# Experts run in two parts, the first on twelve quads' tokens from the end of the attention on

## The reference, cut to what matters

```python
x = x + xattn(layernorm(x), ctx)              # (64, 128, 128), 16 heads of 8
y = layernorm(x)                              # 8192 tokens
scores = softmax(y @ gate_w.T)                # 8 experts
sel = top_k(scores + expert_bias, 2)
for each chosen (token, expert e):
    r = y[token] * scores[token, e]
    out[token] += (silu(r @ w1[e]) * (r @ w3[e])) @ w2[e]     # 128 -> 352 -> 128
x = x + out
```

## Time and profile before

| | us |
|---|---|
| median of 3 runs | 871.06 |
| the profiled execution | 866.23 |
| its span | 864.2 |
| TensorE busy | 720.2 |
| GpSimd busy | 437.7 |
| VectorE busy | 494.9 |
| ScalarE busy | 419.3 |

### The profile page before, as it was taken

How to read it: one execution, slowest core, us unless ns; L and a number is a source line. 1 busy time by engine, 2 the same in 40 slices (tenths; PEclk the granted TensorE clock), 3 DMA queues, 4 the chain that set the end, 5 groups by cost and what they waited for, 6 DMA issues and landing times.

```text
span 864.2 us, 24903 instructions
## 1 busy us (share of the span) xinstructions
PE 720.2 (83%) x7007; PEld 577.8 (67%) x7008; DVE 494.9 (57%) x1404; ACT 419.3 (49%) x935; POOL 437.7 (51%) x779
## 2 busy tenths in 40 slices
PE   1689999999999999999963359999999999999800
PEld 1356677666777776676642158989999899898800
DVE  2446667675777776777743425555555555554536
ACT  1246677676677776776551024444444444443300
POOL 6311127665667675665566724555555545445510
PEclk9969999998999999999995769999999999999965
DMA  2445455565666656655300112212121222212179
GB/s 57 142 118 144 130 143 157 136 178 164 162 174 162 169 135 159 164 153 157 75 27 32 59 34 58 59 55 58 58 61 52 59 57 55 61 52 58 38 268 315
DMA packets 99774, 94.84 MB, mean 110 GB/s; under 512 B 15015, under 2 KB 89385, under 8 KB 99632
## 3 DMA queue, kind: packets, MB, share of 16 engines
q1 hardware_dynamic: 82832, 72.81, 31.5%
q0 software_dynamic: 8416, 16.86, 5.7%
q10 hardware_dynamic: 8448, 4.20, 1.6%
HBM read 55.00 MB, written 39.26 MB: 109 GB/s over the span
## 4 chain that ended last, share of the span: by engine, by line
PE 59%; DMA 12%; issue 9%; SPq 6%; DVE 6%; POOL 5%; ACT 2%; DVEq 0%; POOLq 0%; ACTq 0%
PE m_b L1190 7%; PE score_b L999 7%; PE u_b L1039 6%; PE score_b L957 4%; PE turned_b L1021 4%; PE score_b L198 3%; POOL expert_rows L440 3%; DMA head_rows<-qk 2%; SPq L236 2%; DVE nm L530 2%; PE m_a L1180 2%; PE turned_b L200 2%; PE turned_b L199 2%; PE score_b L200 2%; PE turned_b L198 2%
## 5 line engine op out<-in xcount | busy, mean ns | idle before, releaser
L471 POOL DMA_INDIRECT expert_results<-v,where x135 | 132.9, 984 | 156.8 <-DMA expert_results<-v,where 133.7
L530 DVE TENSOR_REDUCE nm<-score_b 128x8 f32<-128x960 f32 x128 | 148.2, 1158 | 96.4 <-PE score_b L999 92.8
L440 POOL DMA_INDIRECT expert_rows<-rows,places x128 | 128.9, 1007 | 71.0 <-POOL rows L434 49.7
L842 ACT ACTIVATE pT<-turned_b 120x1024 f32<-120x1024 f32 x128 | 130.9, 1023 | 61.2 <-PE turned_b L1021 46.4
L921 ACT ACTIVATE v<-score_b 128x352 f32<-128x352 f32 x135 | 62.7, 464 | 116.0 <-PE turned_b L200 114.9
L1190 PE MATMUL m_b<-w_s,v 128*128 (+1 forms) x810 | 115.7, 279 | 0.6 <-ACT v L926 0.6
L1190 PEld LDWEIGHTS m_b<-w_s,v 128*128 128x128 f32 (+1 forms) x810 | 100.9, 191 | 4.2 <-issue 0.8
L999 PEld LDWEIGHTS score_b<-ks,qs 63*128 63x128 f32 x1024 | 68.8, 192 | 37.2 <-issue 37.2
L769 DVE COPY v<-m_a 128x384 f32<-128x384 f32 x67 | 37.4, 558 | 86.4 <-PE m_a L1180 78.7
L999 PE MATMUL score_b<-ks,qs 63*128 63x120 f32 x1024 | 86.6, 290 | 0.0
L1039 PE MATMUL u_b<-pT,v 120*32 120x128 f32 x2048 | 84.8, 285 | 0.3 <-ACT pT L842 0.2
(11 more groups left out here) (140 smaller groups left out, 1498.8 us busy)
## 6 DMA issues: line engine op xcount, KB each, us to landing
head_rows<-qk SPq DMA_DIRECT2D x32, 496.0 KB
qs<-head_rows SPq DMA_DIRECT2D x192, 64.0 KB
ks<-head_rows SPq DMA_DIRECT2D x96, 120.0 KB
v<-expert_rows SPq DMA_DIRECT2D x135, 64.5 KB, 1.8
v<-expert_results SPq DMA_DIRECT2D x16, 512.0 KB, 5.6
x_s<-in_x SPq DMA_DIRECT2D x32, 128.0 KB, 2.8
out<-pT ACTq DMA_DIRECT2D x16, 256.0 KB, 5.9
c_s<-in_ctx_in SPq DMA_DIRECT2D x32, 120.0 KB
```

The lines of the kernel that those rows point to most:

```text
L440: eng.indirect_dma_start(xs_dram, bass.IndirectOffsetOnAxis(ap=places[:, n % 2, u, k:k + 1], axis=0), rows[:, h, k, :], None).then_inc(sca ...
L471: eng.indirect_dma_start(y_dram, bass.IndirectOffsetOnAxis(ap=where[:, q:q + 1], axis=0), y_s[:, q, :], None, bounds_check=2 * T - 1, oob_ ...
L530: eng.tensor_reduce(nm[:, p % 2, :].rearrange("p (a h n u) -> p a h n u", a=2, h=2, u=2)[:, :, h, :, u], score_b[:, :, 0:4 * K].rearrange( ...
L842: eng.activation(pT[0:K, g % 2 * 1024:g % 2 * 1024 + 1024].rearrange("k (a t) -> k a t", a=2), turned_b[0:K, :, :], ACT.Exp).then_inc(c.ex ...
```

## The change

Each engine's program is changed in the same way.

- The tokens are parted: quads 0 to 11 and quads 12 to 15 have their own `expert_rows` and `expert_results`, their own regions, pad rows and counts. The worst case is 103 tiles and 39 tiles, 142 together. `tile_counts(0)` runs in VectorE's pass n = 13 and `tile_rows(0)`, `tile_experts(0)` after pass 14; those of part 1 run in rounds 30 to 32.
- The loops over n end earlier (after 13 on GpSimd and ScalarE, 14 on VectorE, 15 on TensorE), and the steps of the last quads that are left stand in the rounds of the experts: `scatter` in three pieces (`gated_rows` and two `send`), one in a round, for quad 13 from round -2, quad 14 from round 14, quad 15 from round 27; `turn_normed`, `logits`, `ranks` and the choice of experts for quads 14 and 15 in rounds 3 to 32.
- The first tiles' tokens use other PSUM banks (`xT_b(t)`), `hT_b` is one bank for two, `y_b` is `u_b`; the attention's tail keeps `m_b` and `m_c`. The two fills of `hT_b` with zeros and the 30 matmuls of `keep_clock_up` in front of the experts are gone.
- Rounds are written out, with no hardware loop. TensorE loads the registers of the next four tiles behind `up(r)` for r % 4 == 3, into `near`.
- From round 108 on the results of part 0 are loaded, added and stored, one of 12 in every second round; the last four loads come behind part 1. `add_up` adds both results to `x2` in place, and `store` reads `x2`; the loads go to the space of `qs`.

The diff, cut (lines that only move or rename are left out):

```diff
@@ -39,8 +39,13 @@
     QUADS, PAIRS, HALVES = B // 4, B // 2, 2 * B
     HC = (HID + P - 1) // P
     CHUNK = [min(P, HID - c * P) for c in range(HC)]
-    CAP = T + P
-    NT = 2 * T // P + E - 1
+    EARLY = QUADS * 3 // 4
+    PART = EARLY, QUADS - EARLY
+    T_OF = [4 * S * n for n in PART]
+    CAP = [n + P for n in T_OF]
+    NT_OF = [2 * n // P + E - 1 for n in T_OF]
+    NT, NT0 = sum(NT_OF), NT_OF[0]
...
+        old_q = qs[:, :, :, :, :, :].rearrange("p r s e b q -> p (r s e b q)").bitcast(F32)
+        both = old_q[:, 0:YB * LG * 2 * D].rearrange("p (y g k d) -> p y g k d", y=YB, g=LG, k=2)
...
-        hT_b, y_b, xT_b = (u_b, m_a), m_b, m_c
+        hT_b, y_b = m_a, u_b
+        def xT_b(t):
+            return score_b[:, 1, t * P:t * P + P] if t < 2 else turned_b[:, 1, 0:P] if t == 2 else m_c[:, 0:P]
...
-                    r = E * CAP + (n - 5) * P
                     if n == 5:
                         eng.wait_ge(pad_rows, 2)
-                    eng.dma_start(xs_dram[r:r + P, :], padding[:, :]).then_inc(spare_r, 16)
+                    for i in range(2):
+                        r = E * CAP[i] + (n - 5) * P
+                        eng.dma_start(xs_dram[i][r:r + P, :], padding[:, :]).then_inc(spare_r, 16)
...
+            def pad_ends(i):
+                eng.wait_ge(ended, i + 1)
+                eng.load(end_rows, ends[0:1, i, :])
+                for reg in end_rows:
+                    row = bass.RuntimeValue.of_register_unchecked(reg).with_bounds(min_val=0, max_val=E * CAP[i] - P)
+                    eng.dma_start(xs_dram[i][bass.ds(row, P), :], padding[:, :]).then_inc(padded, 16)
+            def tiles_ready(i):
+                for h in range(2):
+                    eng.wait_ge(scat[h], 16 * 4 * sum(PART[:i + 1]))
+                eng.wait_ge(padded, 16 * E * (i + 1))
+                eng.wait_ge(spare_r, 16 * 2 * (E - 1))
+                eng.wait_ge(table, 2 * (i + 1))
...
+                i = t >= NT0
+                if t == 0:
+                    eng.wait_ge(c.PV, HALVES - 12)
...
+            def results_there(i):
                 for q in range(4):
-                    tile_load(r * 4 + q, q)
-            for t in range(last, NT):
-                tile_load(t, t % 4)
-            for q in range(4):
-                if due((NT - q + 3) // 4): eng.wait_ge(tile_out[q], 16 * ((NT - q + 3) // 4))
-            def y_load(n, q):
-                if due(n - YB + 1): eng.wait_ge(added, n - YB + 1)
-                src = y_dram.rearrange("(p b k) d -> p b k d", p=P, k=2)[:, bass.ds(n * LG, LG), :, :]
+                    eng.wait_ge(tile_out[q], 16 * ((sum(NT_OF[:i + 1]) - q + 3) // 4))
+            def y_load(n):
+                q, i = n % YB, n >= EARLY
+                if n < YB: eng.wait_ge(c.ST, HALVES)
+                if due(n - YB + 1): eng.wait_ge(total, n - YB + 1)
...
+            pad_ends(0)
+            tiles_ready(0)
+            for t in range(NT):
+                if t == NT0 - 12:
+                    pad_ends(1)
+                if t == NT0:
+                    tiles_ready(1)
+                tile(tile_load, t)
+                if t == NT0 + 5:
+                    results_there(0)
+                if t >= NT0 + 5 and (t - NT0 - 5) % 2 == 0:
+                    at(y_load, (t - NT0 - 5) // 2, EARLY)
+            results_there(1)
+            for n in range(EARLY, QUADS):
+                y_load(n)
...
+            def send(b, k):
+                n, u, h = b // 4, b % 4, b % 2
+                if k == 0:
+                    eng.wait_ge(c.places, n + 1)
+                    eng.wait_ge(c.rows, b + 1)
+                    eng.wait_ge(c.placed, b + 1)
+                    settled(eng)
+                eng.indirect_dma_start(
+                    xs_dram[n >= EARLY], bass.IndirectOffsetOnAxis(ap=places[:, n % 2, u, k:k + 1], axis=0),
+                    rows[:, h, k, :], None).then_inc(scat[h], 16)
...
+            for r in range(-2, NT + 2):
+                tile(results, r - 2)
+                if r == 3:
+                    rstd2(QUADS - 1)
+                for n, first in ((QUADS - 3, -2), (QUADS - 2, 14), (QUADS - 1, 27)):
+                    if first <= r < first + 12:
+                        part_of_sending(12 * n + r - first)
+                tile(keep_places, r + 1)
...
+            for n in range(-6, QUADS - 1):
...
+                if n == EARLY + 1:
+                    tile_counts(0)
+            tile_rows(0)
+            tile_experts(0)
...
-            def add_up(n, q):
...
+            def add_up(n):
+                q, whole = n % YB, x2[:, n * LG:n * LG + LG, :]
                 eng.wait_ge(y_in[q], (n - q) * 4 + 16)
-                if due(n - q): eng.wait_ge(stored[q], (n - q) * 4)
-                eng.tensor_tensor(tot[:, q, :, :], both[:, q, :, 0, :], both[:, q, :, 1, :], ALU.add).then_inc(added, 1)
+                eng.tensor_tensor(whole, whole, both[:, q, :, 0, :], ALU.add).then_inc(added, 1)
                 eng.wait_ge(added, n + 1)
-                eng.tensor_tensor(tot[:, q, :, :], tot[:, q, :, :],
-                                             x2[:, bass.ds(n * LG, LG), :], ALU.add).then_inc(total, 1)
-            for n in range(YB):
-                add_up(n, n)
-            with eng.Fori(1, B // LG // YB) as r:
-                for q in range(YB):
-                    add_up(r * YB + q, q)
+                eng.tensor_tensor(whole, whole, both[:, q, :, 1, :], ALU.add).then_inc(total, 1)
...
+                for k, first in ((n, 6), (m, 18)):
+                    if r == first:
+                        logit_max(k)
+                        logit_shift(k)
+                    if r == first + 2: gate(k)
+                    if r == first + 3: pick(k)
+                    if r == first + 4: index(k)
+                    if r == first + 6: place(k)
+                if r == 30: tile_counts(1)
+                if r == 31: tile_rows(1)
+                if r == 32: tile_experts(1)
...
+            gate_parts(k)
+            tile(tokens_low, 0)
+            tile(tokens_low, 1)
+            place(k)
+            denominators(2 * n + 1)
+            divide(2 * n + 1)
+            residual(2 * n)
+            for r in range(NT + 2):
+                tile(hidden, r - 1)
+                if r == 1:
+                    residual(PAIRS - 1)
+                    stats2(B - 4)
+                    stats2(B - 3)
+                tile(tokens_low, r + 2)
+                tile(gated, r)
+                last_quads(r)
+                if r >= NT0 + 7 and (r - NT0 - 7) % 2 == 0:
+                    at(add_up, (r - NT0 - 7) // 2, EARLY)
...
+            exps(HALVES - 2)
+            exps(HALVES - 1)
+            heads(PAIRS - 2)
+            context(PAIRS - 1)
+            tile(tokens_high, 0)
+            tile(tokens_high, 1)
+            for r in range(NT + 2):
+                tile(silu, r)
+                if r == 0: heads(PAIRS - 1)
+                tile(tokens_high, r + 2)
+                tile(result, r - 2)
+                if r == 1:
+                    normalise2(4 * n)
+                    normalise2(4 * n + 1)
+                if r == 2:
+                    normalise2(4 * n + 2)
+                    normalise2(4 * n + 3)
+                if r == 4: normed(n)
+                if r == 7: router(n)
+                if r == 9:
+                    normalise2(4 * m)
+                    normalise2(4 * m + 1)
+                if r == 10:
+                    normalise2(4 * m + 2)
+                    normalise2(4 * m + 3)
+                if r == 16: normed(m)
+                if r == 19: router(m)
+                if r >= NT0 + 8 and (r - NT0 - 8) % 2 == 0:
+                    at(store, (r - NT0 - 8) // 2, EARLY)
...
-            eng.wait_ge(ended, 1)
-            keep_clock_up(30)
-            eng.wait_ge(table, 4)
+            eng.wait_ge(table, 2)
             eng.wait_ge(ffn_weights, 16 * HC)
             eng.wait_ge(weights_l, PIECES)
-            old = [eng.alloc_register(f"old_expert{n}") for n in range(4)]
-            now = [eng.alloc_register(f"expert{n}") for n in range(4)]
...
+            near = [eng.alloc_register(f"expert{n}") for n in range(8)]
+            def expert(t, group):
+                return eng.snap(near[t - group + 4], min_val=0, max_val=E - 1)
+            def experts(group):
+                if group < NT0 <= group + 4:
+                    eng.wait_ge(table, 4)
+                eng.load(near, t_exp[0:1, group:group + 8])
...
+                if t == 0: eng.wait_ge(c.max, HALVES)
+                if t == 2: eng.wait_ge(c.exp, HALVES)
+                if t == 3: eng.wait_ge(c.x2, PAIRS)
+                if t >= 4: eng.wait_ge(f.xT_l, t)
...
-            def experts(t, q):
-                if q == 0:
-                    eng.load(old + now, t_exp[0:1, bass.ds(t, 8)])
-            def round_(r, u):
-                tile(experts, r, u)
-                tile(up, r, u)
-                tile(turn_hidden, r, u, 1)
```

(24 more changed lines are left out.)

289 lines of the change are left out of this document (156 added, 133 removed).

## The result

The kernel after takes 836.78 us (median of 4 runs, 831.76 to 838.87), the kernel before beside it 869.29 (864.42 to 871.38): ratio 0.9625, interval 0.956 to 0.969. That is faster, inside the range of 789 to 838 by 1.2 us, and 27 us above the likeliest value of 810. The profiled run of after took 838.87 us, its span is 837.1.

What follows compares the result with a forecast made beforehand. TensorE was taken to bound attention and experts, a chain the gap between, transfers the end. `up(39)` at 552.2 + 219.8 + 8 + 2 + 8.7 + 12.2 gave 802.9 us of span, 810 as median; range 789 to 838.

Steps and rivals of the forecast that it cites:

- The attention's end: Last mix of the attention at 448.0 us, plus 1.0 for `tile_counts(0)`; the table's 4.6 us on VectorE taken as hidden.
- `up(0)`, rounds 0 and 1: Start of the experts: `up(0)` 3.0 us behind the attention's end, at 452.0; rounds 0 and 1 take 5.0 us.
- Sending rounds: Rounds 2 to 38, with the last quads' sends on GpSimd: 2.48 us for each sending round, 95.2 us in all.
- Register load: Every fourth expert round: loading behind `up` leaves 0.3 us of the 0.8 us stall; bounds 0 and 0.8.
- Rounds 39 to 102: Expert rounds between the sends and the results: mean interval 2.155 us, 137.9 us in all.
- Results beside part 1: Every second round from 108: part 0's results cost 0.7 us for each of 12, 8 us; bounds 0 and 22.
- The end: After the last `up`: 8.7 us to the first result load, then 12.2 us with four loads for sixteen.
- B: Rival: nothing is covered; register stall stays 0.8 us and GpSimd keeps long gaps in sending rounds; 843 us, chance 0.10.
- A: Rival: in the expert rounds the sends cost nothing and TensorE covers the register load; 792 us, chance 0.13.
- C: Rival: tile loads queue behind part 0's results, 1.6 + 0.3 us for each of 12; 824 us, chance 0.10.
- D: Rival: tile 0 isn't there at the attention's end, 15 to 20 us of the gap remain; 828 us, chance 0.05.
- E: Rival: slower, as TensorE's clock falls to 1.2 GHz in sending and result rounds; up to 900 us, chance 0.03.

Runs made afterwards that it cites:

- a2: The kernel after, unchanged, run again as a yardstick in a slower group: 868.24 us, ratio to before 0.972.
- e3: The kernel after with part 0's table made in six steps behind the attention's last six maxima on VectorE: 844.26 us, ratio to before 0.970.
- g1: After with eight tile and result buffers, thinned sends, early table steps, later first result load, and extra GpSimd work in six quiet rounds: 790.97 us, ratio to before 0.904.
- e1: The kernel before with expert rounds and tile loads written out instead of looped, register loads still ahead of `up`: 871.78 us against 871.43, ratio 0.998.
- e2: The kernel after with part 1's eight end pads spread, one ahead of every second tile load from 83 on: 840.42 us, ratio to before 0.964.
- e4: The kernel after with all result loads, additions and stores behind the last round: 854.04 us, ratio to before 0.978.
- e6: The kernel after with part 0's twelve result loads issued from ScalarE's queue instead of SP's: rounds 103 to 141 took 100.2 us (100.8 in a2).
- e7: The kernel after with the register load back ahead of the group's first `up`: 875.28 us, a single execution.
- d1: The kernel after with eight tile buffers and eight columns of `where` instead of four: 832.73 us where a2 took 868.24, ratio to before 0.934.

## Why the prediction was right, and where it was off

The sign and the mechanism were right: the gap is filled, the results overlap, the range held. That it held, by 1.2 us, is in part luck: nearly all misses go the same way, and in a2's group the same kernel took 868. The profiled run of after has a span of 837.1 where the sum gave 802.9. Step by step:

- *The attention's end.* Forecast 449.0, measured 453.7. Of the 5.7 us by which it is later than in before, 2.5 had been lost before group 116 (421.28 for 418.74), by the changing stretches at half clock as far as can be told. The other 3.1 stand between group 116 and the last `mix`, where the clock was 0.84 and in before 0.94 (418.74 to 447.38). The table had been "hidden" for nothing, from VectorE's idle share in the earlier trace rows; by what is queued behind it it can have cost up to 1.7 us, which e3 doesn't separate from the clock.
- *`up(0)`, rounds 0 and 1.* 2.9 us behind the last `mix` for 3.0, and 5.5 for 5.0. Right.
- *Sending rounds.* 103.1 for 95.2. Mis-sized, and the loads themselves hardly are the reason: from issue to last packet they took 1.7 us on the mean, in before's rounds 1.5. But they were issued late. Of the eleven loads that TensorE waited for, seven had taken 1.6 to 1.7 us and four 2.4 to 2.6. SP waited for the copy of the places ahead of nearly every one (62.4 us), so the loop was longer than I took it to be. One step was missing from it: the copy of tile t waits for the scatter of tile t - 4 to land, 2.3 us behind its start in a case within S (480.84 to 483.10), and that landing makes up over half of the chain from 660 to 720. What each step of the loop adds in S stays open. Some 7 us of S went at half the clock besides. That the four-buffer loop sets this stage was right: with eight of each it took 85.4 (g1, in which a part of the sends has moved to Q, where they cost nothing).
- *Register load.* I left 0.3 us a group; nothing is left (2.08 in a2), so 8 us of the sum were too much. Written out, the 0.8 us are 0.4 even where the load stays ahead of `up` (e1). The loop's turn I had rightly put at nothing: 2.09 us from `up(61)` to `up(62)`, with the turn between them. The Trainium skill (Runtime: NRT & Kernel Launch, Instruction fetch mechanics) has a stall for a taken branch to outside the fetched window. No run here shows such a stall.
- *Rounds 39 to 102.* 150.5 for 137.9, in spite of that. The failed step is one that is absent: `pad_ends(1)`, in the diff, moves eight issues past SP's tile loads. I had its 5.0 us in my hand for part 0 and didn't charge it for part 1. It cost 7.5 (e2), more than its issues take; for 6.8 us around the wait the clock was at half. The rest are single rounds of 2.5 to 3.8 us, 6 us in Q; with eight buffers, in g1, they are gone. Instruction fetches may be behind them (after has 127 fetch packets, before 78), but that was only argued: g1 has 126, and no long round in Q.
- *Results beside part 1.* I took 0.7 us for each of 12, 8 in all, with bounds 0 and 22. Measured with and without (e4): 16.2. Term mis-sized: 8.8 are waits, and the rest is time that TensorE was busy longer at the lower clock, for which I had no term. Nor is it every second round: rounds 107, 113 and 125 took 5.1, 6.3 and 4.7 us, and 12 of the 26 rounds from 105 to 130 stayed under 2.2. And 5 of 36 tile loads took over 2.5 us to their last packet, one 4.5, which I had named as a sign of being wrong. The sum by the Trainium skill (DMA: Bandwidth & Descriptors, Queues, rings and completion order) was 19, nearer than mine; but its place, the order in SP's ring, isn't what e6 shows, where another engine's queue cost the same.
- *The end.* 20.8 for 20.9. Right.

Of the rivals, B came nearest in time, 843, by what didn't happen: its register stall is gone (e7, a2). A's covered load was right. C, results that delay tile loads, was there in size but not through the queue. D was wrong: tile 0 was in time. E was wrong in size, since the granted clock's mean stayed at 0.93 to 1.00 in the stages. But the clock did stand at half around the longest waits, for 24 us in all, and my sum charged nothing for that. The early signs held: TensorE was busy for 8.8 of the 12 us from 448 to 460, and the sending rounds stood at 2.79 on the mean.

All the misses but the attention's and the register load's are one: I priced each thing that can delay a tile load by itself, and took the loop's slack as next to nothing for one of them only. d1 changed just the number of buffers, of tiles and of their places together, and took back 34 us in one step; which of the two did it isn't told apart.
